# A Mamba block beside an expert layer: expert rows that carry gate and token, expert tiles spread over chunks 1 to 13, low parts on VectorE

## The chip, the cores and the metric

The kernel runs on one core of a Trainium2 chip. The metric is the device time of one execution in microseconds. In what follows VectorE is DVE in the rows, ScalarE is ACT, TensorE is PE (PEld for its weight loads), GpSimd is POOL and SyncE, which issues most DMAs, is SP.

## What is computed

32 sequences of 256 tokens with 128 channels (8192 tokens) are normalized; the result is the input plus the outputs of two branches. All is float32.

```python
xn = layernorm(x)
# branch 1: Mamba, 4 heads of 64 channels, 16 states
x, z  = split(xn @ in_proj_w.T)
x     = silu(causal_conv4(x)); dt_r, B, C = x_proj(x)
delta = softplus(dt_proj(dt_r) + dt_proj_b)
s_t   = s_{t-1} * exp(delta_t * A) + (delta_t * x_t) * B_t
y     = (sum over states of s_t * C_t + x * Dskip) * silu(z)
out1  = y @ out_proj_w.T
# branch 2: 8 experts, each takes at most 1024 tokens (top 1)
gates = softmax(xn @ Wg); e = argmax(gates); slot = place in the expert's queue
hidden = relu(expert_in[e] @ W1[e] + b1[e])
out2[token] = gate * (hidden @ W2[e] + b2[e])[slot]     # 0 when the queue is full
result = x_in + out1 + out2
```

## The kernel before

After a start (normalization, weights, routing) the tokens are worked in 16 chunks of 512 tokens (2 sequences), and a chunk in 32 slots, w = 0 to 31; slots 0 to 15 belong to half 0 of the inner channels, slots 16 to 31 to half 1. Each slot handles 8 channels with 16 states each, on the 128 partitions:

- TensorE spreads delta times x and delta over the states (`spread_du`, L1177, and `spread_delta`, L1184, both float32r) two slots ahead. `spread_delta(w)` goes into one of three banks and waits for scan w-3; `spread_du(w)` goes into one of two and waits for VectorE's product of slot w-2.
- ScalarE makes the decay, exp (L757).
- VectorE makes u = du * B (L897) one slot ahead and the scan of the slot (L967).
- GpSimd multiplies the scan's result by C (L573). In chunk 0 VectorE does three of four of these products (L974), in chunk 15 one of four.
- TensorE sums four slots' products over the states (`sum_quad`, L1199).

Between those stands all other work. Each engine's order is written out: the tables STAGE_A, D_1, OUT_PROJ and FFN give the slot in which TensorE makes each tile, and ScalarE reads it two slots, VectorE one slot, after the last part. All these tiles share two PSUM banks (`misc`) in turn, and `claim` makes TensorE wait until the tile before last was read. STAGE_A is the next chunk's input: x (convolution as four products, L1109), z, bc (B and C), v (L1122) and D (delta, four products, L1130 to L1133), for either half. `outp` is the last chunk's output product (L1142), which VectorE adds to `acc` (`add_out`, L867). The two gate steps of each half (L855, L859) are VectorE's.

Delta goes out as a high and a low part: GpSimd multiplies it by x (`scale_x`, L529) and clears the first step (L533), ScalarE rounds the pair to float32r (`split_high`, L721), and `split_low` takes the difference: on GpSimd in chunks 1 to 8 (L539), on VectorE otherwise (L903). SP then stacks both parts for TensorE (L429).

The experts: in chunk 0 GpSimd scatters the 8192 normalized rows to the experts' queues in HBM with 64 indirect DMAs (L580). Chunks 1 to 8 each work one expert as two halves of 512 rows: transposes `xt` (L1155), four hidden tiles `h` (L1159, ScalarE's relu L732), one output tile `o` in two parts (L1166), which VectorE reads with the bias added (`expert_out`, L875) and SP stores. In chunks 9 to 15 GpSimd gathers the results in token order, 8 indirect DMAs a chunk and 8 more at the end (L549), and VectorE adds each 128-row tile, times its gate, to `acc` (`combine`, L888).

```python
FFN = {"xt0": (18,), "xt1": (19,), "h00": (20,), "h01": (20,), "h02": (21,), "h03": (23,),
       "o0": (24, 24, 25, 25), "h10": (26,), "h11": (26,), "h12": (27,), "h13": (27,),
       "o1": (29, 29, 30, 30)}
SOFTPLUS = {"act": (2, 3, 4, 5), "scale": (9,), "zero": (10,), "low": (13,), "high": (13,)}
```

The numbers of SOFTPLUS are slots after tile v of that half.

Of the kernel before, what the change touches and what calls it, by code (L numbers as in the profile page):

```python
# [1300 lines left out]
```

## Time and profile before

| | us |
|---|---|
| median of 3 runs | 1230.49 (1229.86 to 1234.8) |
| the profiled execution's own time | 1231.65 |
| its span, first to last instruction | 1229.8 |
| VectorE busy | 1065.7 (87%) |
| TensorE busy (weight loads) | 1013.1 (476.6) |
| GpSimd busy | 858.1 (70%) |
| ScalarE busy | 733.5 (60%) |
| mean granted TensorE clock | 0.913 |

The profiled execution is 1.9 us longer than its span; that part lies outside the instructions. A busy TensorE is not one at its peak, since its matmuls are pipelined and their ends are modelled. The 16 chunks begin where the scan of their slot 0 begins: at 93.6, 185.2, 257.6, 325.4, 393.3, 461.1, 529.0, 598.4, 666.3, 734.1, 802.9, 871.3, 939.6, 1007.9, 1076.2 and 1144.4 us.

### The profile page before, as it was taken

To read this page: it belongs to the slowest core of one execution; us is meant where nothing else is said; L and a number is where in the kernel's file an instruction comes from. 1 tells how busy PE (TensorE), PEld (TensorE's weight loads), DVE (VectorE), ACT (ScalarE), POOL (GpSimd) and SP (SyncE) were. 2 spreads that over 40 slices of the span, in tenths; PEclk is the share of its full clock that TensorE was granted. 3 is DMA by queue.
4 is the path that set the end of the run, shared out by engine and by line. 5 is a ranking of instruction groups with operands and counts; after the bars stand their busy time and mean duration, and the time that the engine had idled before them with its cause. 6 is when DMAs were issued, how large, how long until landed. Compare 5 with 4: busy or idle time off the path is not lost.

```text
span 1229.8 us, 12361 instructions
## 1 busy us (share of the span) xinstructions
PE 1013.1 (82%) x3821; PEld 476.6 (39%) x3821; DVE 1065.7 (87%) x1331; ACT 733.5 (60%) x1117; POOL 858.1 (70%) x708
## 2 busy tenths in 40 slices
PE   0755858989999899999899998798888888788775
PEld 0522314444445454444445453243343424243322
DVE  7648968889898979889898989989898989999996
ACT  2563635767585766757685866656664756556421
POOL 2335788767676867677676769687777878787755
PEclk9988878999999999999999998888898979898776
DMA  6542425243533424342534323442434342344311
GB/s 159 160 86 69 98 77 133 58 97 70 120 69 79 103 51 111 78 111 39 117 69 104 85 61 77 86 86 54 87 66 92 80 83 60 80 86 83 75 31 34
DMA packets 81089, 103.36 MB, mean 84 GB/s; under 512 B 13280, under 2 KB 51072, under 8 KB 81024
## 3 DMA queue, kind: packets, MB, share of 16 engines
q1 hardware_dynamic: 76928, 94.18, 35.4%
q0 software_dynamic: 4096, 8.40, 2.3%
q8 instruction: 31, 0.51, 0.2%
q14 instruction: 34, 0.28, 0.1%
HBM read 18.66 MB, written 16.78 MB: 29 GB/s over the span
## 4 chain that ended last, share of the span: by engine, by line
PE 40%; DVE 27%; issue 19%; ACT 6%; POOL 5%; DMA 1%; SPq 1%; POOLq 0%; DVEq 0%; ACTq 0%
DVE u_sb L897 11%; DVE s_sb L967 8%; PE bank L1199 5%; PE bank L1166 5%; PE bank L1184 5%; PE bank L1177 5%; PE bank L1122 3%; PE bank L1109 3%; PE bank L1130 3%; POOL s_sb L573 2%; PE bank L1142 2%; PE bank L1131 2%; PE bank L1132 2%; DVE g_sb L855 2%; DVE g_sb L859 1%
## 5 line engine op out<-in xcount | busy, mean ns | idle before, releaser
L573 POOL TENSOR_TENSOR s_sb<-s_sb,c_of 128x512 f32<-128x512 f32 x480 | 628.1, 1314 | 270.5 <-DVE s_sb L967 266.9
L967 DVE TENSOR_TENSOR_SCAN s_sb<-bank,u_sb 128x512 f32<-128x512 f32 x512 | 619.3, 1210 | 0.0
L757 ACT ACTIVATE bank<-bank,a_neg 128x510 f32<-128x510 f32 x512 | 333.6, 659 | 255.9 <-PE bank L1184 255.0
L897 DVE TENSOR_TENSOR u_sb<-bank,b_of 128x512 f32<-128x512 f32 x512 | 345.2, 674 | 100.8 <-PE bank L1177 100.8
L1177 PE MATMUL bank<-dsp,sel_d 128*128 128x512 f32 x512 | 311.1, 608 | 40.7 <-DVE u_sb L897 21.9
L1184 PE MATMUL bank<-dsp,sel_d 128*128 128x512 f32 x512 | 239.9, 469 | 82.6 <-DVE s_sb L967 77.2
L1177 PEld LDWEIGHTS bank<-dsp,sel_d 128*128 128x128 f32 x512 | 103.1, 201 | 240.4 <-DVE u_sb L897 140.2
L1184 PEld LDWEIGHTS bank<-dsp,sel_d 128*128 128x128 f32 x512 | 104.7, 205 | 196.2 <-DVE s_sb L967 168.9
L1199 PE MATMUL bank<-s_sb,con 128*32 128x512 f32 x1024 | 157.2, 690 | 12.6 <-POOL s_sb L573 8.6
L1109 PE MATMUL bank<-xnT,wx 128*128 128x512 f32 x256 | 129.0, 598 | 0.0
L580 POOL DMA_INDIRECT expert_in<-xn,put_at x64 | 65.4, 1022 | 18.0 <-issue 17.7
L549 POOL DMA_INDIRECT xn<-expert_out,take_now x64 | 65.9, 1030 | 10.6 <-issue 9.1
L721 ACT ACTIVATE hi<-dd 128x1024 fp32r<-128x1024 f32 x32 | 33.9, 1058 | 61.4 <-POOL dd L533 61.4
L1166 PE MATMUL bank<-xn 128*128 128x128 f32 x512 | 63.7, 278 | 7.2 <-ACT xn L732 7.2
L1166 PEld LDWEIGHTS bank<-xn 128*128 128x128 f32 x512 | 60.8, 191 | 18.1 <-ACT xn L732 10.4
L1122 PE MATMUL bank<-xs,bcw 128*64 128x512 f32 x64 | 43.8, 773 | 28.8 <-ACT xs L672 28.8
L529 POOL TENSOR_TENSOR dd<-dd,xs 128x512 f32<-128x512 f32 x32 | 40.8, 1276 | 34.5 <-ACT dd L715 34.5
L1159 PE MATMUL bank<-xn 128*128 128x512 f32 x128 | 64.4, 605 | 0.3
L1109 PEld LDWEIGHTS bank<-xnT,wx 128*128 128x128 f32 x256 | 47.5, 190 | 27.6 <-issue 22.8
L715 ACT ACTIVATE dd<-bank,small 128x512 f32<-128x512 f32 x32 | 22.0, 688 | 57.4 <-PE bank L1133 57.4
L732 ACT ACTIVATE xn<-bank,b_now 128x512 f32<-128x512 f32 x64 | 43.1, 689 | 14.5 <-PE bank L1159 13.9
L1142 PEld LDWEIGHTS bank<-wzo,g_sb 128*128 128x128 f32 x256 | 40.8, 235 | 18.8 <-issue 16.7
(140 smaller groups left out, 1032.1 us busy)
## 6 DMA issues: line engine op xcount, KB each, us to landing
b_of<-bc SPq DMA_DIRECT2D x64, 256.0 KB, 5.5
c_of<-bc SPq DMA_DIRECT2D x64, 256.0 KB, 5.9
dsp<-hi SPq DMA_DIRECT2D x64, 256.0 KB, 4.2
dsp<-dd SPq DMA_DIRECT2D x64, 256.0 KB, 4.7
expert_in<-dd SPq DMA_DIRECT2D x8, 512.0 KB, 6.3
xn<-expert_in SPq DMA_DIRECT2D x8, 512.0 KB, 5.6
xn<-L_ffn_W SPq DMA_DIRECT2D x16, 256.0 KB, 4.8
expert_out<-xn SPq DMA_DIRECT2D x16, 256.0 KB, 2.4
```

What stands on the lines that cost most here:

```text
L549: pool.indirect_dma_start(back[:, n, :], None, eout[:, :], bass.IndirectOffsetOnAxis(ap=take_now[:, n:n + 1], axis=0),).then_inc(S["back_l ...
L573: pool.tensor_tensor(s_now, s_now, c_of[:, hf, hh, :], ALU.mult).then_inc(S["p_ready"], 1)
L580: pool.indirect_dma_start(ein[:, :], bass.IndirectOffsetOnAxis(ap=put_at[:, i:i + 1], axis=0), xn[:, i, :], None).then_inc(S["scattered"], 16)
L757: act.activation(d, d, ACT.Exp, scale=a_neg[:, k:k + 1]).then_inc(S["decay_ready"], 1)
L897: dve.tensor_tensor(u_sb[:, w % U_RING, :], du_ps[w % 2][:, :], b_of[:, hf, head_of(w), :], ALU.mult).then_inc(S["u_ready"], 1)
L967: dve.tensor_tensor_scan(s_sb[:, w % S_RING, :], decay_of(w)[:, :], u_sb[:, w % U_RING, :], 0.0, ALU.mult, ALU.add).then_inc(S["scan_done" ...
L1109: mm = pe.matmul(t[:, :], wx[:, hf, part, :], xnT[:, seqs, part:part + SEQ], start=(part == 0), stop=(part == TAPS - 1))
L1122: pe.matmul(t[0:4 * NS, :] if name[0] == "b" else t[:, :], w[:, hf, :], xs_of(ch, hf), start=True, stop=True).then_inc(S["misc_pe"], 1)
L1166: mm = pe.matmul(t[:, part * P:(part + 1) * P], hT[:, f, part * P:(part + 1) * P], w2_sb[:, f, :], start=(f == 0), stop=(f == FT - 1))
L1177: pe.matmul(du_ps[w % 2][:, :], sel_d[:, group_of(w), :, :].rearrange("k n d -> k (n d)"), dsp[:, hf, head_of(w), 1, :], start=True, stop= ...
L1184: pe.matmul(decay_of(w)[:, :], sel_d[:, group_of(w), :, :].rearrange("k n d -> k (n d)"), dsp[:, w // UNITS, head_of(w), 0, :], start=True ...
L1199: mm = pe.matmul(y_ps[q * 32:(q + 1) * 32, :], con[:, K_SUM + 32 * r:K_SUM + 32 * (r + 1)], s_sb[:, (QUADS * k + q) % S_RING, :], start=(r ...
```

## The change

- **Rows carry their gate and token.** A row of `xn` and of an expert's queue has 130 columns: 128 channels, gate, token number as an integer. Queues are filled first with zero rows whose token number points behind the result (`fill`).
- **Token order by scatter.** ScalarE reads an expert's output tile, now 128 rows wide and one PSUM tile each, and multiplies by the gate (`expert_out`); the bias b2 is added by a product with a row of ones. GpSimd writes each of the 64 tiles to `moe` in token order with an indirect DMA (`put_rows`). SP loads `moe` back in eight pieces after the last expert. GpSimd adds them for chunks 0 to 12 (`add_moe`, one every fourth slot from slot 26 of chunk 13), TensorE for chunks 13 to 15, as four products with the identity inside `out_proj`. The gathers, `combine` and `take_indices` are gone.
- **Tiles in a table of their own.** 144 expert tiles (16 halves of xt, four h, four o) go one by one to the 12 slots of FFN_AT in chunks 1 to 13; two experts' weights and rows are in SBUF at a time. Each tile names its bank, and relu reads its bias without VectorE's copy of it. Stage A and the softplus chain have new slots: D is in two slots, x ends in slot 4.
- **Low parts.** All but the very first are VectorE's, in slot 21 for half 0 and slot 3 of the chunk itself for half 1.

```diff
-LAST_GATHER = 22
+ROWX = DM + 2
...
-STAGE_A = {"z0": (1,), "x0": (2, 4, 5, 7), "bc0": (8,), "v0": (11,), "z1": (12,), "x1": (15, 16, 17, 17),
-           "D0": (18,), "bc1": (25,), "v1": (26,)}
-
-D_1 = (0,)
-OUT_PROJ = (9, 10)
...
+STAGE_A = (
+    ("x0", 1, (0, 1, 3, 4), "act", 6), ("z0", 0, (4,), "act", 5.5), ("bc0", 1, (7,), "bc", 9),
+    ("v0", 1, (9,), "act", 11), ("x1", 1, (11, 12, 13, 14), "act", 16), ("z1", 0, (13,), "act", 15.5),
+    ("D0", 0, (16, 16, 17, 17), "act", 19), ("bc1", 1, (21,), "bc", 23), ("v1", 1, (23,), "act", 25),
+    ("D1", 0, (29, 29, 31, 31), "act", 33))
+FIRST_D1 = (0, (0, 0, 1, 1), "act", 3)
+OUT_PROJ = (1, (18, 19), "dve", 20)
+
+
+FFN_AT = ((2, 0), (7, 0), (9, 0), (11, 0), (19, 0), (21, 0), (23, 0), (25, 0), (26, 1), (27, 0), (28, 1), (30, 1))
+FFN_SKIP = 4
+FFN_LAST_CHUNK = 13
+
+
+SOFTPLUS = ({"act": (11, 12, 13, 14), "scale": (17,), "zero": (18,), "high": (22,), "low": (20,), "low_dve": (21,)},
+            {"act": (25, 26, 27, 28), "scale": (31,), "zero": (32,), "high": (36,), "low": (34,), "low_dve": (35,)})
...
+MOE_ADD_FROM, MOE_ADD_STEP, MOE_ADDS = 13 * 32 + 26, 4, 13
...
-        def low_by_pool(ch):
-
-            return has_ffn(ch)
...
+        def low_by_pool(of):
+
+            return of == 0
...
+            def put_rows(x):
+
+                e, th, q = x.of, x.hf, x.k
+                if x[1:4] == (0, 0, 0):
+                    pool.wait_ge(S["moe_filled"], 16 * EXP)
+                pool.wait_ge(*tile_read(*x[0:4]))
+                pool.indirect_dma_start(moe[:, :],
+                                        bass.IndirectOffsetOnAxis(
+                                            ap=xe[:, e % 2, th * CT + q, DM + 1:ROWX].bitcast(U32), axis=0),
+                                        eo[:, th, q, :], None).then_inc(half_put(e, th)[0], 16)
+
+            def add_moe(k):
+
+                pool.wait_ge(*tile_read("outp", k, 0, 0))
+                pool.wait_ge(S[f"back_loaded{k * CT // GROUP}"], 16)
+                rows = acc[:, k * CT:(k + 1) * CT, :]
+                pool.tensor_tensor(rows, rows, back[:, k * CT:(k + 1) * CT, :], ALU.add).then_inc(S["moe_added"], 1)
...
+            def expert_out(x):
+
+                if x.k == 0 and (x.of, x.hf) != (0, 0):
+                    act.wait_ge(*half_put(x.of - 1 + x.hf, 1 - x.hf))
+                act.wait_ge(S["misc_pe"], tile_made(*x[0:4]))
+                act.activation(eo[:, x.hf, x.k, :], misc[x.bank][:, 0:DM], ACT.Copy,
+                               scale=xe[:, x.of % 2, x.hf * CT + x.k, DM:DM + 1]).then_inc(S["misc_act"], 1)
...
+                    if more:
+                        mm = pe.matmul(t[:, i * P:(i + 1) * P], ident, back[:, ch * CT + i, :],
+                                       start=False, stop=True)
```

How the order moves on TensorE, in chunk 4 from slot 17 on (L1177 and L1184, now L1154 and L1161, are the spreads that open a slot; L1199, now L1176, the sums; L1109 is x, L1155 a transpose of expert rows, L1130 to L1133, now L1089 and L1091, the four products of D, L1103 the output product). Before:

```order
L1177 MATMUL bank<-dsp,sel_d 128x512
L1184 MATMUL bank<-dsp,sel_d 128x512
L1109 MATMUL bank<-xnT,wx 128x512 x2
L1177 MATMUL bank<-dsp,sel_d 128x512
L1184 MATMUL bank<-dsp,sel_d 128x512
L1199 MATMUL bank<-s_sb,con 32x512 x4
L1155 MATMUL bank<-con,xn 128x128 x4
L1130 MATMUL bank<-sp_e,con 128x512
L1131 MATMUL bank<-sp_r,con 128x512
L1132 MATMUL bank<-sp_a,con 128x512
L1133 MATMUL bank<-hi,neg_id 128x512
L1177 MATMUL bank<-dsp,sel_d 128x512
```

And now, from slot 16 on:

```order
L1154 MATMUL bank<-dsp,sel_d 128x512
L1161 MATMUL bank<-dsp,sel_d 128x512
L1089 MATMUL bank<-sp_e,con 128x512
L1089 MATMUL bank<-sp_r,con 128x512
L1154 MATMUL bank<-dsp,sel_d 128x512
L1161 MATMUL bank<-dsp,sel_d 128x512
L1089 MATMUL bank<-sp_a,con 128x512
L1091 MATMUL bank<-hi,neg_id 128x512
L1154 MATMUL bank<-dsp,sel_d 128x512
L1161 MATMUL bank<-dsp,sel_d 128x512
L1176 MATMUL bank<-s_sb,con 32x512 x4
L1103 MATMUL bank<-wzo,g_sb 128x128 x4
```

The sum, the transposes and the whole of D stood in one slot between two pairs of spreads; D now lies in slots 16 and 17, ahead of the sum.

On VectorE, chunk 4, slots 20 to 22 (L897, now L895, is u; L967, now L960, the scan; L855 and L859, now L875 and L879, the gate steps). Before:

```order
L897 TENSOR_TENSOR u_sb<-bank,b_of 128x512
L967 SCALAR_TENSOR_TENSOR s_sb<-bank,u_sb 128x512
L855 SCALAR_TENSOR_TENSOR g_sb<-xs,small,bank 128x512
L897 TENSOR_TENSOR u_sb<-bank,b_of 128x512
L967 SCALAR_TENSOR_TENSOR s_sb<-bank,u_sb 128x512
L859 TENSOR_TENSOR g_sb<-g_sb,zs 128x512
```

And now:

```order
L960 SCALAR_TENSOR_TENSOR s_sb<-bank,u_sb 128x512
L886 TENSOR_TENSOR acc<-bank,acc 128x512
L895 TENSOR_TENSOR u_sb<-bank,b_of 128x512
L960 SCALAR_TENSOR_TENSOR s_sb<-bank,u_sb 128x512
L875 SCALAR_TENSOR_TENSOR g_sb<-xs,small,bank 128x512
L901 TENSOR_TENSOR dd<-dd,hi 128x1024
L895 TENSOR_TENSOR u_sb<-bank,b_of 128x512
```

`add_out` (L886) comes one slot ahead of the first gate step, and the low part (L901) right behind that step.

On GpSimd, from the middle of chunk 3 (L573, now L596, are the products by C; L529, now L542, `scale_x`; L539 the low part; L566 a put). Before:

```order
L573 TENSOR_TENSOR s_sb<-s_sb,c_of 128x512
L533 MEMSET dd 128x2
L573 TENSOR_TENSOR s_sb<-s_sb,c_of 128x512 x3
L539 TENSOR_TENSOR dd<-dd,hi 128x1024
L573 TENSOR_TENSOR s_sb<-s_sb,c_of 128x512 x11
L529 TENSOR_TENSOR dd<-dd,xs 128x512
```

And now:

```order
L596 TENSOR_TENSOR s_sb<-s_sb,c_of 128x512
L546 MEMSET dd 128x2
L596 TENSOR_TENSOR s_sb<-s_sb,c_of 128x512 x2
L566 DMA moe<-xn 8704x128
L596 TENSOR_TENSOR s_sb<-s_sb,c_of 128x512 x2
L566 DMA moe<-xn 8704x128
L596 TENSOR_TENSOR s_sb<-s_sb,c_of 128x512 x2
```

The two low parts of a chunk leave GpSimd, and the puts, each of which waits for ScalarE's copy, stand between its products.

## Rows read from the trace of the kernel before

**Rows 1.** The page: busy time of TensorE to GpSimd; granted clock in 40 slices.

```profile
PE 1013.1 (82%) x3821; PEld 476.6 (39%) x3821; DVE 1065.7 (87%) x1331; ACT 733.5 (60%) x1117; POOL 858.1 (70%) x708
...
PEclk9988878999999999999999998888898979898776
```

**Rows 2.** Stretches: from:to and length, busy (count) by engine, granted clock, DMA share, GB/s.

```profile
93.60:185.20 91.60, 58.09 (x163) 22.98 (x162) 74.95 (x93) 41.38 (x63) 66.92 (x65) 0.80 0.32 79
185.20:257.60 72.40, 66.41 (x277) 33.77 (x276) 60.66 (x73) 47.70 (x74) 54.46 (x44) 0.96 0.39 90
257.60:734.10 476.50, 443.35 (x1919) 227.68 (x1918) 420.35 (x505) 328.52 (x505) 339.49 (x266) 1.00 0.39 86
734.10:1076.20 342.10, 288.55 (x930) 121.97 (x929) 316.18 (x402) 206.29 (x310) 264.43 (x220) 0.87 0.38 78
1076.20:1144.40 68.20, 57.54 (x187) 24.31 (x186) 62.97 (x81) 41.30 (x63) 52.66 (x44) 0.88 0.38 78
1144.40:1213.80 69.40, 50.69 (x147) 19.05 (x145) 67.83 (x86) 21.65 (x33) 47.05 (x39) 0.72 0.23 51
```

**Rows 3.** VectorE's groups, 257.6 to 734.1: busy us, mean ns, idle before, releaser.

```profile
L897 DVE TENSOR_TENSOR u_sb<-bank,b_of 128x512 f32<-128x512 f32 x225 | 151.4, 673 | 46.1 <-PE bank L1177 46.1
...
L875 DVE TENSOR_TENSOR xn<-bank,xn 128x512 f32<-128x512 f32 x14 | 9.5, 676 | 9.5 <-PE bank L1166 9.5
```

**Rows 4.** VectorE's groups, 734.1 to 1076.2.

```profile
L897 DVE TENSOR_TENSOR u_sb<-bank,b_of 128x512 f32<-128x512 f32 x161 | 108.8, 676 | 23.3 <-PE bank L1177 23.3
L888 DVE SCALAR_TENSOR_TENSOR acc<-xn,gate,acc 128x128 f32<-128x128 f32 x40 | 13.0, 326 | 0.0
...
L867 DVE TENSOR_TENSOR acc<-bank,acc 128x512 f32<-128x512 f32 x5 | 3.5, 692 | 2.6 <-PE bank L1142 2.6
```

**Rows 5.** VectorE in order of time, chunk 4: start, us, instruction, idle before.

```profile
393.27 1.21 DVE L967 TENSOR_TENSOR_SCAN s_sb<-bank,u_sb 128x512 f32<-128x512 f32 x1
394.40 0.67 DVE L897 TENSOR_TENSOR u_sb<-bank,b_of 128x512 f32<-128x512 f32 x1
394.99 1.21 DVE L967 TENSOR_TENSOR_SCAN s_sb<-bank,u_sb 128x512 f32<-128x512 f32 x1
...
431.63 0.69 DVE L897 TENSOR_TENSOR u_sb<-bank,b_of 128x512 f32<-128x512 f32 x1 [2.17 <-PE bank L1177]
```

**Rows 6.** TensorE in order of time, chunk 4, slot 18.

```profile
426.90 1.06 PE L1199 MATMUL bank<-s_sb,con 128*32 128x512 f32 x8
...
428.39 1.02 PE L1130 MATMUL bank<-sp_e,con 128*128 128x512 f32 x2
429.26 1.02 PE L1131 MATMUL bank<-sp_r,con 128*128 128x512 f32 x2
...
431.21 0.39 PE L1177 MATMUL bank<-dsp,sel_d 128*128 128x512 f32 x1
```

**Rows 7.** VectorE's low part and GpSimd in order of time, chunk 9.

```profile
748.62 1.27 POOL L573 TENSOR_TENSOR s_sb<-s_sb,c_of 128x512 f32<-128x512 f32 x1
749.39 1.60 DVE L903 TENSOR_TENSOR dd<-dd,hi 128x1024 fp32r<-128x1024 f32 x1
...
750.06 1.79 POOL L549 DMA_INDIRECT xn<-expert_out,take_now  x1 [0.16 <-issue]
```

**Rows 8.** Chunk 0 and the start of chunk 1: VectorE's wait, GpSimd's scatters.

```profile
167.21 1.23 DVE L903 TENSOR_TENSOR dd<-dd,hi 128x1024 fp32r<-128x1024 f32 x1 [9.07 <-ACT hi L721]
...
191.44 0.96 POOL L580 DMA_INDIRECT expert_in<-xn,put_at  x1 [0.30 <-issue]
```

**Rows 9.** The end, in order of time.

```profile
1212.71 2.32 DVE L967 TENSOR_TENSOR_SCAN s_sb<-bank,u_sb 128x512 f32<-128x512 f32 x2
...
1215.61 2.49 POOL L573 TENSOR_TENSOR s_sb<-s_sb,c_of 128x512 f32<-128x512 f32 x2
...
1218.24 1.93 PE L1199 MATMUL bank<-s_sb,con 128*32 128x512 f32 x8 [5.86 <-POOL s_sb L573]
...
1221.85 3.56 PE L1142 MATMUL bank<-wzo,g_sb 128*128 128x128 f32 x16 [1.68 <-DVE g_sb L859]
```

More of the change, by code:

```diff
@@ L53 @@
 GROUP = 8
-FIRST_FFN, FIRST_COMBINE = 1, 9
 EPS = 1e-5
@@ new lines, in expert_tiles, with out_tiles @@
+        def expert_tiles():
+            at = [(c * SLOTS + w, b) for c in range(1, FFN_LAST_CHUNK + 1) for w, b in FFN_AT][FFN_SKIP:]
+            kinds = [("xt", 0)] + [("h", f) for f in range(FT)] + [("o", q) for q in range(CT)]
+            names = [(kind, e, th, k) for e in range(EXP) for th in range(2) for kind, k in kinds]
+            return [Tile(kind, e, th, k, b, (t,), "act", t + 2) for (kind, e, th, k), (t, b) in zip(names, at)]
+        def out_tiles():
+            bank_, slots, by, read = OUT_PROJ
+            tiles = [Tile("outp", c, 0, 0, bank_, tuple((c + 1) * SLOTS + w for w in slots), by,
+                          (c + 1) * SLOTS + read) for c in range(CHUNKS - 1)]
+            end = CHUNKS * SLOTS
+            return tiles + [Tile("outp", CHUNKS - 1, 0, 0, 0, (end, end), by, end)]
@@ new lines, in bass_mamba_moe, with tile_bank @@
+        prior = {}
+        for b in range(2):
+            same = [x for x in plan if x.bank == b]
+            for x, y in zip(same, same[1:]):
+                assert x.slots[-1] <= y.slots[0], (x, y)
+                prior[y[0:4]] = x[0:4]
+        parts_at, reads_at = {}, {}
+        for x in plan:
+            for part, t in enumerate(x.slots):
+                parts_at.setdefault(t, []).append((x, part))
+            reads_at.setdefault(x.read, []).append(x)
+        def tile_bank(*key):
+            return misc[find[key].bank]
@@ new lines, in tile_made, with tile_read @@
+        def tile_made(*key):
+            return made[key]
+        def tile_read(*key):
+            return read[key]
+        def low_by_pool(of):
+            return of == 0
+        events = {}
+        for of in range(CHUNKS):
+            for hf in range(HALVES):
+                slots = {k: tuple((of - 1) * SLOTS + w for w in v) for k, v in SOFTPLUS[hf].items()}
+                if of == 0:
+                    if hf == 0:
+                        continue
+                    slots = {k: (w,) for k, w in FIRST_SOFTPLUS.items()}
+                by_dve_ = of == 0 or not low_by_pool(of)
+                slots.pop("low" if by_dve_ else "low_dve")
+                for what, at in slots.items():
+                    for step, t in enumerate(at):
+                        events.setdefault((what, t), []).append((of, hf, step))
```

742 lines of the change are left out of this document (324 added, 418 removed).

## The prediction

> **What bounds the kernel now.** I read the page's first lines, then stretches by chunk, then VectorE's groups, then single slots. VectorE is the busiest engine [rows 1]; its scans and the making of u cannot be skipped, so the question is what it waits for. One slot without a wait is 394.99 - 393.27 = 1.72 us, and an operation over 512 columns takes 0.59 of that (394.99 - 394.40) [rows 5]. That would be 55.0 us a chunk of 32 slots. The stretches [rows 2] give 476.5 / 7 = 68.1 us for chunks 2 to 8 and 342.1 / 5 = 68.4 us for chunks 9 to 13, almost the same length with different contents. In chunks 2 to 8 VectorE waits for TensorE's next spread and for the expert's output tile: (46.1 + 9.5) / 7 = 7.9 us a chunk [rows 3]. In chunks 9 to 13 it waits (23.3 + 2.6) / 5 = 5.2 us, and spends time on combines [rows 4]. The wait has a place. In slot 18 TensorE goes from the sum at 426.90 through transposes and D to the next spread at 431.21, 4.3 us in one piece [rows 6], and VectorE idles 2.17 us [rows 5]. So a slot may hold 4.3 - 2.2 = 2.1 us of TensorE work beyond its spreads before VectorE feels it, if TensorE came to it on time.
>
> A difference of 0.5% is about what a measurement of this kernel can tell from no change.
>
> **Chunks 2 to 13.** I take VectorE's work without waits from both kinds of chunk, since they must agree.
>
> From chunks 2 to 8: 68.1 - 7.9 = 60.2. Two output tiles leave for ScalarE, 2 x 0.59 = 1.2. Two low parts come from GpSimd, 1.23 each [rows 8], 1.15 in sequence as records overlap by 0.08. That is 60.2 - 1.2 + 2.3 = 61.3.
>
> From chunks 9 to 13: 68.4 - 5.2 = 63.2. Eight combines go, 0.326 each [rows 4], 0.26 in sequence, 2.1 in all; the low parts are VectorE's already. That is 61.1. I use 61.0, since the copies of b1 and of the indices, some tenth each, go too.
>
> Onto this come waits. *TensorE's piles.* One float32 product of 512 columns takes 0.87 (429.26 - 428.39), a sum of four 1.0 [rows 6], a 128-column product at the lower clock 3.56 / 8 = 0.445 [rows 9], so 0.22 at the full one, and an output tile with its bias five of them, 1.1. The 144 expert tiles, 18 a chunk before, are now 11 or 12 a chunk, never two in a slot. The largest run left is slots 14 to 19: x and sum 1.9, none, half of D 1.7, rest of D 1.1, sum and output product 1.9, output product and tile 2.0, with six pairs of spreads near 0.5 in all 11.6 us, where VectorE takes 10.3. It enters with about 1.5 us from slots 11 to 13, so VectorE, which can bear 2.1, waits about 1 us a chunk. Ends: 0, and 5.2 as in chunks 9 to 13; the value is nearer the lower end since the 4.3 us piece is cut in parts under 2.1.
>
> *GpSimd beside VectorE.* At 749.39 a low part began 0.77 us after GpSimd's product and took 1.60 instead of 1.23; GpSimd's next issue took 1.79 [rows 7] where 0.96 is usual [rows 8]. So these two hold each other up when they overlap. In slot 21 the low part now stands behind a gate step of 0.59, by which time the product of the slot is under way: it must wait 0.7 to 0.8. For the other three places (slots 3, 6 and 22) I take 0.5 together, as GpSimd may lag after a put. So 1.3 a chunk; ends 0 and 5.1 (below).
>
> Sum: 61.0 + 1.0 + 1.3 = 63.3, twelve times 759.6 against 476.5 + 342.1 = 818.6: **-59.0 us**.
>
> The Trainium skill says of this in "SBUF — State Buffer", section "SBUF: two separate sides", that VectorE, with two inputs in SBUF, and GpSimd take one port pair exclusively for a whole instruction and that the later one fully blocks. That rule speaks against putting low parts on VectorE; the 1.60 us record agrees with it. Taken at its worst it is the second rival; the sum above holds only the overlap that the order makes certain, and a little more.
>
> **What covers the rest.** GpSimd has 32 products at 1.27 [rows 7], two multiplications of the same size and 64 / 13 = 5 puts at 1.27 (0.96 and a gap of 0.30) [rows 8]: 49.5 of 63.3 us a chunk, since two low parts left it. The puts cost nothing while that slack lasts; if it goes, see the third rival. ScalarE takes 11 or 12 tiles in place of 16 large ones in chunks 2 to 8, and was busy 328.5 / 7 = 46.9 of 68.1 us [rows 2]. SP issues the expert's loads ahead of two stacks; their waits are for puts a chunk old. The eight loads of `moe` run from slot 23 of chunk 13; the first sum on GpSimd, three slots on, may wait a few us once.
>
> **Start, chunk 0 and chunk 1.** Nothing before the first scan at 93.6 moves that I can price over 0.3. In chunk 0 GpSimd issues scatters without pause, and VectorE waits for it, 9.07 us in one place [rows 8]. The low part there is now asked for after slot 19, not 23, but the same 64 scatters stand in GpSimd's queue up to 191.44 + 0.96 = 192.4 [rows 8]. After them now come a multiplication and a product, 2 x 1.27, then ScalarE's rounding and VectorE's low part, 1.2 each (the same 1024 columns). Slot 3 of chunk 1 ends at 197.4 at the earliest. The other 28 slots take 48.2, four gate steps and the sum 3.0, one low part 1.2, small gaps 0.8, waits 2.1: chunk 2 begins at 252.7, not 257.6: **-4.9**. Ends: -9 (no wait behind) and +1.5 (the fills of `moe`, 4 MB more, slow the scatters by a tenth, 64 x 0.1).
>
> **Chunk 14** has no expert tile and the lower clock (0.88) of its kind [rows 2]; waits between 1.0 and 5.2, I take 2.5: 61.0 + 2.5 + 1.3 = 64.8, **-3.4**. **Chunk 15** [rows 2]: 61.0, eight products more (4.7), one low part less (1.2), no scan at the end of the stretch (1.1), waits 1.5: 64.9 for 69.4, **-4.5**. **The end**: the last two products began at 1215.61, behind a gather, though the scans are over by 1215.03 [rows 9]; now the second can end by 1216.6, and the sum begins 1.6 us sooner than at 1218.24. The output product has twelve products for eight, 4 x 0.445 = 1.8 more. **0.**
>
> All in all -4.9 - 59.0 - 3.4 - 4.5 = -71.8 us. The profiled execution took 1231.65, 1.85 of it outside its span; it comes to 1159.9. It stands 1.2 us over the median, so **1159 us**, 5.8% faster.
>
> **Rivals.**
> - *TensorE stays the one waited for.* Banks are now fixed by tile, and a late ScalarE read or a lower clock keeps the waits at the 5.2 us of chunks 9 to 13. Against it: the 4.3 us piece is gone; TensorE, with some 58 of 63 us busy, should keep the clock at 1.00, as it did in chunks 2 to 8 and not in chunks 9 to 13 [rows 2]. 4.2 x 12 = 50 more: 1209 us. Chance 0.10.
> - *Low parts and gate products are blocked in full.* Four VectorE operations a chunk with both inputs in SBUF each wait for a whole product of GpSimd, 4 x 1.27 = 5.1 for 1.3: 3.8 x 13 = 49 more, 1208 us. It needs a GpSimd that is always late. This is the rule of the Trainium skill named above ("SBUF — State Buffer") at its worst. Chance 0.05.
> - *The puts stand on the path (slower).* A put waits on GpSimd for ScalarE's copy, and products queue behind it, which TensorE's sums, and through them everything, wait for. In chunk 0 scatters did this [rows 8]. If each put costs VectorE its whole 1.27, that is 64 x 1.27 = 81 us: 1240 us. It decides from 1.2 us a put on, where the gain is used up. Against it: about five puts a chunk, 6.4 us, against 13.8 us of slack. Chance 0.06.
> - *Nothing is waited for.* The spread-out order takes away all waits: 12 x 2.3 and 7 us elsewhere less, 1124 us. Chance 0.10.
>
> The forecast keeps 0.69; its own range is 1140 to 1180. The range reaches down to most of the last rival and up to part of the first two: 1128 to 1200. Faster by over 0.5%: 0.69 + 0.10 + 0.05 + 0.10 = 0.94. The put rival is split, 0.02 within 0.5%, 0.04 slower.
>
> **What would show it.** Right: chunks 2 to 13 of equal length, 62 to 65 us; VectorE's idle time before u down from 46.1 in seven chunks to under 15; low parts in slot 21 at about 1.9 us, those in slot 3 at 1.23; granted clock 1.00 from chunk 2 to 13; TensorE's sums not waiting for GpSimd. Wrong: idle time before u of 4 us or more a chunk (first rival), every low part near 2.4 (second), GpSimd's products without idle time before them in most slots of chunks 1 to 13 (third), or a chunk under 61.5 us (fourth). Chunk 2 beginning much off 252.7 would show my reading of chunk 0 wrong.

## The result and the profile after

| | before | changed |
|---|---|---|
| median, us | 1230.17 | 1197.48 (1188.55 to 1200.14, 4 runs) |
| ratio to before | | 0.9713, 95% interval 0.9657 to 0.9769 |
| the profiled execution's own time, us | 1231.65 | 1198.12 |
| its span, us | 1229.8 | 1196.3 |
| mean granted clock | 0.913 | 0.920 |

All times are of fast runs; one of the four runs of experiment 12 took 3093.73 us and is left out.

The change makes the kernel 2.9% faster: 33 us, where 71 were forecast. The time lies at the upper end of the range; the direction was right, the size was not.

The page of the changed kernel, busy time and granted clock in 40 slices:

```profile
PE 1016.6 (85%) x3973; PEld 495.0 (41%) x3973; DVE 1077.1 (90%) x1251; ACT 754.5 (63%) x1181; POOL 846.6 (71%) x707
...
PEclk9897858998999998999999899999989999999766
```

It answers to [rows 1]. The stretches of the changed kernel, cut at the same places as [rows 2] (here chunks 2 to 13 are one row):

```profile
95.30:181.90 86.60, 65.37 (x169) 24.89 (x167) 77.39 (x93) 41.77 (x63) 64.05 (x62) 0.74 0.50 130
181.90:257.00 75.10, 63.01 (x230) 29.81 (x228) 61.47 (x72) 45.03 (x71) 55.59 (x47) 0.89 0.40 94
257.00:1055.30 798.30, 735.30 (x3023) 370.04 (x3022) 751.93 (x853) 557.49 (x880) 602.23 (x496) 0.97 0.37 82
1055.30:1118.20 62.90, 54.61 (x198) 23.84 (x196) 61.86 (x72) 41.89 (x63) 53.94 (x45) 0.95 0.45 99
1118.20:1181.70 63.50, 49.89 (x151) 19.27 (x149) 62.53 (x76) 21.56 (x33) 38.75 (x29) 0.68 0.30 71
```

Against the forecast: chunk 2 begins at 257.0 and not 252.7 (+4.3). Chunks 2 to 13 take 798.3 and not 759.6 (+38.7). Chunk 14 takes 62.9 for 64.8, chunk 15 up to the last scan 63.5 for 64.9, and what follows the last scan 14.6 for 16.0 (together -4.7). The sum is 38.3 us, and 1158.05 forecast for the span plus 38.3 is the 1196.3 measured. So the miss is in chunks 2 to 13. VectorE's groups there (busy, mean ns, idle before):

```profile
L960 DVE TENSOR_TENSOR_SCAN s_sb<-bank,u_sb 128x512 f32<-128x512 f32 x384 | 464.3, 1209 | 5.6 <-ACT bank L779 5.6
L895 DVE TENSOR_TENSOR u_sb<-bank,b_of 128x512 f32<-128x512 f32 x385 | 257.8, 670 | 41.4 <-PE bank L1154 40.1
L901 DVE TENSOR_TENSOR dd<-dd,hi 128x1024 fp32r<-128x1024 f32 x24 | 49.4, 2058 | 0.4
```

Waits are (41.4 + 5.6) / 12 = 3.9 us a chunk for a forecast of 1.0. The low parts are (49.4 - 24 x 1.23) / 12 = 1.66 us longer for a forecast of 1.3. With the 61.0 us of work without waits that is 66.6, and 798.3 / 12 is 66.5, so the 61.0 us were right. Waits for TensorE were (46.1 + 9.5) / 7 = 7.9 a chunk before in chunks 2 to 8 [rows 3] and 5.2 in chunks 9 to 13 [rows 4]. They shrank, but did not go. The 5.6 us before scans are waits for ScalarE, 0.47 us in slot 17 of each chunk, behind the loading of a table (chunk 7):

```profile
620.73 1.28 ACT L693 ACT_TABLE_LOAD   x1
622.03 1.81 ACT L779 ACTIVATE bank<-bank,a_neg 128x510 f32<-128x510 f32 x3
...
622.72 1.22 DVE L960 TENSOR_TENSOR_SCAN s_sb<-bank,u_sb 128x512 f32<-128x512 f32 x1 [0.47 <-ACT bank L779]
```

The kernel before had no idle time before its scans. No run tests this wait.

Three readings of the trace say where most of the rest sits. First, slot 3 of chunk 8. In order of time, VectorE and then GpSimd:

```profile
661.98 1.21 DVE L960 TENSOR_TENSOR_SCAN s_sb<-bank,u_sb 128x512 f32<-128x512 f32 x1
663.29 3.65 DVE L901 TENSOR_TENSOR dd<-dd,hi 128x1024 fp32r<-128x1024 f32 x1
666.86 0.68 DVE L895 TENSOR_TENSOR u_sb<-bank,b_of 128x512 f32<-128x512 f32 x1
...
662.12 3.72 POOL L596 TENSOR_TENSOR s_sb<-s_sb,c_of 128x512 f32<-128x512 f32 x3
```

GpSimd, late after a put and a clearing, has three products to catch up. The low part's record begins at 663.29, during the first of them, and ends 1.1 us after the third. The low parts of slot 3 are such in chunks 2, 5, 8 and 11, and 1.50 us in most others; those of slot 21 are 1.9 us throughout. Meanwhile TensorE idles for want of the next u, and its clock falls. Stretches of 6 us around that place (granted clock is the third number from the end):

```profile
658.00:664.00 6.00, 6.00 (x31) 3.31 (x30) 5.89 (x8) 3.82 (x7) 5.44 (x6) 1.00 0.87 164
664.00:670.00 6.00, 4.09 (x10) 1.52 (x9) 6.00 (x5) 4.21 (x6) 4.90 (x4) 0.98 0.43 90
670.00:676.00 6.00, 5.57 (x17) 2.16 (x17) 6.00 (x9) 3.03 (x5) 3.81 (x4) 0.50 0.48 118
```

TensorE was busy 4.09 of 6 us, and then stood at half speed, 1.2 GHz. Second, slot 28 of chunk 7, in order of time:

```profile
645.32 0.65 ACT L723 ACTIVATE sp_e<-sp_e 128x512 f32<-128x512 f32 x1
...
645.84 0.74 ACT L725 ACTIVATE hi<-sp_x,small 128x512 fp32r<-128x512 f32 x1
646.45 0.70 ACT L748 ACTIVATE xn<-bank,b1c 128x512 f32<-128x512 f32 x1
...
647.30 0.46 PE L1126 MATMUL bank<-xn,one_row 1*128 1x128 f32 x2 [2.64 <-ACT xn L748]
...
649.12 0.69 DVE L895 TENSOR_TENSOR u_sb<-bank,b_of 128x512 f32<-128x512 f32 x1 [2.38 <-PE bank L1154]
```

The output tile needs the relu (L748) of the hidden tile one slot ahead of it. ScalarE first does two softplus operations, TensorE stands 2.64 us, and the next spread, behind it in TensorE's order, comes 2.38 us late. Third, the end of every chunk. Chunk 3, TensorE and then VectorE:

```profile
384.49 0.80 PE L1154 MATMUL bank<-dsp,sel_d 128*128 128x512 f32 x1
385.80 0.50 PE L1161 MATMUL bank<-dsp,sel_d 128*128 128x512 f32 x1 [0.51 <-DVE s_sb L960]
386.23 1.07 PE L1176 MATMUL bank<-s_sb,con 128*32 128x512 f32 x8
387.23 1.12 PE L1121 MATMUL bank<-xn 128*128 128x512 f32 x2
387.79 0.79 PE L1154 MATMUL bank<-dsp,sel_d 128*128 128x512 f32 x1
...
388.62 0.69 DVE L895 TENSOR_TENSOR u_sb<-bank,b_of 128x512 f32<-128x512 f32 x1 [1.17 <-PE bank L1154]
```

TensorE waits for the scan that has just ended (three decay banks do not divide 32 slots), then has a sum and a tile before the spread that VectorE needs. This idle time, 1.07 to 1.17 us, stands in slot 31 of eleven of the twelve chunks.

### The profile page after: what moved, and what is told of

Read it like the earlier page. It is cut to its first block, busy times and chain, and to the rows that moved or that the text cites. A ratio compares the mean times of both kernels' runs of the same rounds, so it can differ in the third digit from the quotient of the medians.

```text
span 1196.3 us, 12669 instructions
## 1 busy us (share of the span) xinstructions
PE 1016.6 (85%) x3973; PEld 495.0 (41%) x3973; DVE 1077.1 (90%) x1251; ACT 754.5 (63%) x1181; POOL 846.6 (71%) x707
## 4 chain that ended last, share of the span: by engine, by line
PE 34%; DVE 30%; issue 18%; ACT 9%; POOL 6%; DMA 1%; SPq 1%; POOLq 0%; ACTq 0%; DVEq 0%
DVE u_sb L895 11%; DVE s_sb L960 11%; PE bank L1161 5%; PE bank L1176 4%; PE bank L1129 4%; PE bank L1154 4%; PE bank L1069 4%; POOL expert_in L603 3%; DVE dd L901 3%; PE bank L1080 3%; PE bank L1089 2%; PE bank L1121 2%; ACT bank L779 2%; PE bank L1126 2%; DVE g_sb L875 1%
## 5 line engine op out<-in xcount | busy, mean ns | idle before, releaser
L596 POOL TENSOR_TENSOR s_sb<-s_sb,c_of 128x512 f32<-128x512 f32 x480 | 634.1, 1329 | 221.3 <-DVE s_sb L960 216.8
L960 DVE TENSOR_TENSOR_SCAN s_sb<-bank,u_sb 128x512 f32<-128x512 f32 x512 | 618.7, 1209 | 6.6 <-ACT bank L779 6.6
L895 DVE TENSOR_TENSOR u_sb<-bank,b_of 128x512 f32<-128x512 f32 x512 | 342.8, 669 | 60.5 <-PE bank L1154 59.0
L1154 PE MATMUL bank<-dsp,sel_d 128*128 128x512 f32 x512 | 324.7, 634 | 44.7 <-DVE u_sb L895 31.1
L1161 PE MATMUL bank<-dsp,sel_d 128*128 128x512 f32 x512 | 233.4, 456 | 59.9 <-DVE s_sb L960 57.8
L1154 PEld LDWEIGHTS bank<-dsp,sel_d 128*128 128x128 f32 x512 | 103.0, 201 | 225.5 <-DVE u_sb L895 115.8
L1161 PEld LDWEIGHTS bank<-dsp,sel_d 128*128 128x128 f32 x512 | 103.7, 203 | 175.7 <-DVE s_sb L960 136.6
L1176 PE MATMUL bank<-s_sb,con 128*32 128x512 f32 x1024 | 151.3, 666 | 14.8 <-POOL s_sb L596 11.8
L1069 PE MATMUL bank<-xnT,wx 128*128 128x512 f32 x256 | 132.2, 601 | 0.0
L542 POOL TENSOR_TENSOR dd<-dd,xs 128x512 f32<-128x512 f32 x32 | 40.8, 1275 | 55.6 <-ACT dd L732 55.5
L566 POOL DMA_INDIRECT moe<-xn x64 | 67.9, 1061 | 15.1 <-issue 8.6
L901 DVE TENSOR_TENSOR dd<-dd,hi 128x1024 fp32r<-128x1024 f32 x31 | 60.6, 1956 | 17.5 <-ACT hi L738 17.0
L1129 PE MATMUL bank<-xn 128*128 128x128 f32 x512 | 75.5, 291 | 0.0
L1121 PE MATMUL bank<-xn 128*128 128x512 f32 x128 | 69.5, 626 | 4.3 <-ACT xn L742 4.3
L1129 PEld LDWEIGHTS bank<-xn 128*128 128x128 f32 x512 | 62.9, 194 | 7.8 <-issue 0.2
L748 ACT ACTIVATE xn<-bank,b1c 128x512 f32<-128x512 f32 x64 | 44.4, 694 | 21.0 <-PE bank L1121 20.5
L756 ACT ACTIVATE xn<-bank,xn 128x128 f32<-128x128 f32 x64 | 23.6, 369 | 41.0 <-PE bank L1129 41.0
```

Source lines behind the costliest of these rows:

```text
L596: pool.tensor_tensor(s_now, s_now, c_of[:, hf, hh, :], ALU.mult).then_inc(S["p_ready"], 1)
L895: dve.tensor_tensor(u_sb[:, w % U_RING, :], du_ps[w % 2][:, :], b_of[:, hf, head_of(w), :], ALU.mult).then_inc(S["u_ready"], 1)
L901: dve.tensor_tensor(lo, dd, hi.bitcast(F32), ALU.subtract).then_inc(S["lo_ready"], 1)
L960: dve.tensor_tensor_scan(s_sb[:, w % S_RING, :], decay_of(w)[:, :], u_sb[:, w % U_RING, :], 0.0, ALU.mult, ALU.add).then_inc(S["scan_done" ...
L1069: mm = pe.matmul(t[:, :], wx[:, hf, part, :], xnT[:, seqs, part:part + SEQ], start=(part == 0), stop=(part == TAPS - 1))
L1121: mm = pe.matmul(t[:, :], w1_sb[:, b, x.k * P:(x.k + 1) * P], xeT, start=True, stop=True)
```

## Experiments

Each kernel was timed beside the kernel before on the same chip; that one took 1234.78, 1233.86 and 1232.74 us in the three series (experiments 1 to 4, 5 to 8, 9 to 12). "The changed kernel" is 1197.48, from a series of its own in which the kernel before took 1230.17; it was not timed again. The differences below are of medians. Taken from the ratios instead, experiment 1 gains 8.6 us and not 4.5, experiment 2 24.2 and not 20.9, and the others move by 2.1 us at most.

**1. The decay banks dealt out by the running count.**

```diff
-        def decay_of(w):
-            return decay[w % len(decay)]
+        def decay_of(t):
+            return decay[t % len(decay)]
...
-                last = w - 2 if w >= 3 else (-1, 0, -2)[w]
-                wait(pe, "scan_done", per_chunk(ch, SLOTS, last))
+                t = ch * SLOTS + w
+                wait(pe, "scan_done", t - 2)
```

> The changed kernel with the three decay banks dealt out by the running count of scans, not by the slot in the chunk. Now 32 is no multiple of 3, so the decay spreads issued in slots 30 and 31 wait for the scan that has just begun and not for the one before it. Theory A (fixed places: VectorE's 3.45 us of waits a chunk for TensorE in chunks 2 to 13 sit in a few slots, each with a cause of its own; in slot 31 it is this order): the 1.2 us of idle time before u in slot 31 go in 15 chunks, idle time before u falls from 40.1 to about 26 us in chunks 2 to 13, 1180 us, 1.4% less than the changed kernel. Theory B (TensorE's amount of work is the bound, the place does not matter): the wait turns up in slots 0 to 4, idle time before u stays over 36, 1194 to 1198 us.

Measured: 1193.0 us (1185.7 to 1202.6), ratio 0.9643 (0.9606 to 0.9679). The wait of slot 31 halves, from 1.1 to 0.6 on average, but idle time before u in chunks 2 to 13 is 43.0 us: more stands in slots 27 and 28. By this total and by its time the run is near theory B, though the wait did not turn up in slots 0 to 4. It decides little: its interval and the changed kernel's (0.9657 to 0.9769) overlap, and the profiled execution was the slowest of the four. The clock of the stretch was 0.96, a little under the changed kernel's 0.97 (experiment 9 takes this up).

**2. Both low parts later.**

```diff
-SOFTPLUS = ({"act": (11, 12, 13, 14), "scale": (17,), "zero": (18,), "high": (22,), "low": (20,), "low_dve": (21,)},
-            {"act": (25, 26, 27, 28), "scale": (31,), "zero": (32,), "high": (36,), "low": (34,), "low_dve": (35,)})
+SOFTPLUS = ({"act": (11, 12, 13, 14), "scale": (17,), "zero": (18,), "high": (22,), "low": (20,), "low_dve": (23,)},
+            {"act": (25, 26, 27, 28), "scale": (31,), "zero": (32,), "high": (36,), "low": (34,), "low_dve": (36,)})
```

> The changed kernel with VectorE's low parts asked for in slot 23 instead of 21 and slot 4 instead of 3, where ScalarE's high part has long been ready and no gate step stands between the scan and the low part. Theory A (a low part is long when GpSimd's product is under way as it is asked for): it now starts right behind the scan, level with GpSimd's product; mean of the low parts from 2.06 down to 1.3 to 1.6 us, none at 3.6, 24 x 0.6 = 14 us less in chunks 2 to 13, 1182 us. Rival C (GpSimd gets the port first whenever its product starts together with VectorE's low part): every low part at 1.9 or more, 1190 to 1200 us; the 3.6 us ones (four) go all the same, 4 x 1.7 = 7.

Measured: 1176.58 us (1171.84 to 1177.14), ratio 0.9516 (0.9492 to 0.9541): 20.9 us less than the changed kernel. VectorE's low parts in chunks 2 to 13 of this kernel:

```profile
L901 DVE TENSOR_TENSOR dd<-dd,hi 128x1024 fp32r<-128x1024 f32 x24 | 31.3, 1304 | 0.0
```

That is 49.4 - 31.3 = 18.1 us. Rival C falls: where the low part stands right behind the scan, VectorE gets in ahead of GpSimd's product, in 20 of the 24 places; the other four take 1.8 us. The stretch of chunks 2 to 13 is 16.9 us shorter. Idle time before u stayed (42.6 us for 41.4), so the gain is the low parts' own time. The clock of the stretch rose from 0.97 to 0.98.

**3. Small expert tiles.** For every expert tile TensorE makes only this (its waits stay):

```diff
+                pe.matmul(t[:, 0:32], ident, ident[:, 0:32], start=True, stop=True).then_inc(S["misc_pe"], 1)
```

> The changed kernel with every expert tile on TensorE cut to one product of 32 columns; the tiles' waits, ScalarE's copies and the puts stay. It leaves the experts' arithmetic out. Theory A (fixed places): slot 31 keeps some 1.0 us a chunk for the bank order, the rest of the waits for TensorE falls below 0.5, so 3.45 goes to 1.5, 12 x 2 = 24 us and some 4 in chunk 1 less: 1168 us. Theory B (TensorE's amount of work): waits under 0.5 a chunk, 12 x 3 + 5 = 41 less: 1156 us. If ScalarE's reads alone make the waits: no change, 1190 or more.

Measured: 1166.83 us, ratio 0.9447 (0.9432 to 0.9463). VectorE and the stretch of chunks 2 to 13 in this kernel:

```profile
L895 DVE TENSOR_TENSOR u_sb<-bank,b_of 128x512 f32<-128x512 f32 x385 | 257.7, 669 | 15.6 <-PE bank L1163 14.8
```

```profile
252.90:1025.20 772.30, 683.25 (x2507) 321.43 (x2505) 750.09 (x854) 555.88 (x881) 602.59 (x497) 0.90 0.38 84
```

The time is theory A's, and so is the size of the waits that stay; but they stand in slot 30 (0.6 us a chunk), and slot 31 keeps 0.2 and not 1.0. Idle time before u falls from 41.4 to 15.6 us, but the clock goes down from 0.97 to 0.90: with less to do TensorE gets less often its full clock. So the price of its work is not fixed.

**4. The low parts back on GpSimd.**

```diff
         def low_by_pool(of):
-            return of == 0
+            return True
```

> The changed kernel with all low parts back on GpSimd (slots 20 and 2), one part of the change undone. VectorE loses 2 x 2.06 = 4.1 us a chunk of busy time. Theory A (VectorE's chain with a few fixed waits sets the time): 11 chunks and more at 62.4 to 63.5 instead of 66.5, since GpSimd with 50.2 + 2 x 2.3 = 55 us stays under that: -40 us or so, 1155 us. Theory B (TensorE's amount of work sets it): VectorE only waits more, 1190 us or more. Rival D (GpSimd's low part of over 2 us holds up products, and sums wait for them): 1200 us or more, idle time before TensorE's sums.

Measured: 1193.18 us (1192.91 to 1197.64), ratio 0.9676 (0.9652 to 0.9699): 4 us less than the changed kernel, not 40. Theory B has the time, but no theory had the larger part of the mechanism. VectorE's second gate step in chunks 2 to 13 (658 ns in the changed kernel), and one of them with GpSimd's products, in order of time:

```profile
L879 DVE TENSOR_TENSOR g_sb<-g_sb,zs 128x512 f32<-128x512 f32 x24 | 49.9, 2077 | 0.0
```

```profile
396.67 3.72 POOL L596 TENSOR_TENSOR s_sb<-s_sb,c_of 128x512 f32<-128x512 f32 x3
397.57 3.38 DVE L879 TENSOR_TENSOR g_sb<-g_sb,zs 128x512 f32<-128x512 f32 x1
```

GpSimd's low part (2.37 us) makes it late, and the next VectorE operation with both inputs in SBUF waits until GpSimd has caught up: 49.9 - 15.8 = 34 us take the place of the low parts' 49.4. The waits before u are 55.7 us instead of 41.4. The two together use up what the low parts leave.

**5. The relu of h3 ahead of the softplus step.**

```diff
+                    first = [x for x in reads_at.get(t, []) if x.kind == "h" and x.k == FT - 1]
+                    for x in first:
+                        relu(x)
                     for of, hf_, step in softplus_now(t, "act"):
```

> The changed kernel with one thing moved on ScalarE: where the last hidden tile (h3) of an expert's half and a softplus step fall into one slot, the relu goes first. Theory (pile in slots 25 to 31): in chunks 1, 4, 7 and 10 the output tile of slot 27 follows h3 of slot 26 and TensorE stands up to 2.6 us behind ScalarE's two softplus operations; TensorE's 6.6 us of waits before output tiles go to under 2, VectorE's idle time in slot 28 of those four chunks (2.9, 1.0, 2.4 and 2.4 us) goes to under 0.5 each: 1187 to 1190 us. Rival (TensorE's amount of work; the place only shows it): the time comes back in slots 29 to 31 and 0, no change within 3 us of 1197.

Measured: 1189.06 us (1187.87 to 1193.64), ratio 0.964 (0.962 to 0.966): 8.4 less. Idle time of slot 28 in chunks 1, 4, 7 and 10 is now 1.0, 1.2, 1.2 and 1.1 us instead of 2.9, 1.0, 2.4 and 2.4. Half of it stays, and TensorE still waits 4.4 us for that relu. In this trace something of the rival is seen as well, though not in slots 29 to 31: slot 24 of chunks 5 and 8 now idles 1.7 and 1.4 us, and the total before u is 40.4 for 41.4. The profiled execution was the slowest of the four, at 1193.64 us, so it shows little of the gain; experiment 8 shows it better.

**6. Only the tile of slot 30 small** (the same edit, with the condition `x.slots[0] % SLOTS == 30`).

> The changed kernel with only the expert tile of slot 30 cut to one product of 32 columns (12 or 13 tiles of 144; it leaves their arithmetic out). The banks' order stays. Theory (pile: D in slot 29, sum and tile in slot 30, D in slot 31, 2.6 to 2.8 us of TensorE each with their spreads against 1.72 us of VectorE): the 1.1 us of idle time in slot 31 fall to 0.3 or less, 0.9 x 12 = 11 us less, 1186 us. Rival (the order of the three decay banks alone): slot 31 keeps 0.9 us or more, 1194 to 1198 us.

Measured: 1195.7 us (1189.34 to 1197.96), ratio 0.9692 (0.9651 to 0.9733). Slot 31 falls from 1.1 to 0.4 us, so the tile belongs to that wait. The kernel makes up for little of it: slot 24 of chunks 2, 5 and 11 now idles 1.6 to 1.7 us (0.5 at most in the changed kernel), and the total before u is 35.2 for 41.4. The time is the rival's, the slot the theory's.

**7. Every put twice**, the second time into a tensor that nobody reads (the second issue is shown; the counts of the waits for puts are doubled with it).

```diff
+                pool.indirect_dma_start(moe2[:, :],
+                                        bass.IndirectOffsetOnAxis(
+                                            ap=xe[:, e % 2, th * CT + q, DM + 1:ROWX].bitcast(U32), axis=0),
+                                        eo[:, th, q, :], None).then_inc(half_put(e, th)[0], 16)
```

> The changed kernel with every one of the 64 puts issued a second time, into a second tensor that nobody reads: 64 x 1.06 = 68 us more on GpSimd. If puts stand on the path at their whole price (the slower rival of the prediction): 1255 us or more. If GpSimd's slack covers them: GpSimd has 66.5 - 50.2 = 16.3 us a chunk unused and the second puts take 5 x 1.3 = 6.5, so 1197 to 1203 us, with the low parts of VectorE somewhat longer where GpSimd is later (up to 0.5 x 24 = 12 us, 1209).

Measured: 1213.89 us (1213.56 to 1215.22), ratio 0.9847 (0.9827 to 0.9868): 16.4 us more, 0.26 us a put where the slower rival needed 1.27, and more than the bound of 1209. Chunks 2 to 13 are 17.3 us longer. VectorE now waits up to 2.2 us in slot 3 of eight of these chunks, 14.6 us in all, for the high part, which waits for GpSimd, and its second gate step is longer (21.8 us for 15.8), 2.15 us in slot 6 of four chunks; some low parts are shorter in return:

```profile
L906 DVE TENSOR_TENSOR dd<-dd,hi 128x1024 fp32r<-128x1024 f32 x24 | 45.3, 1889 | 14.6 <-ACT hi L743 14.6
L884 DVE TENSOR_TENSOR g_sb<-g_sb,zs 128x512 f32<-128x512 f32 x24 | 21.8, 910 | 0.0
```

Elsewhere the added work is hidden. From slot 31 to slot 6 of the next chunk GpSimd works half 1's chain of delta beside its products, and there its slack is used up.

**8. Experiments 2 and 5 together.**

> The changed kernel with the later low parts (slots 23 and 4) and the relu of h3 ahead of the softplus step together. If the two gains add: 1176.6 - 9 = 1168 us. If TensorE's amount of work takes over as the bound: 1174 to 1177 us.

Measured: 1166.73 us (1165.72 to 1167.9), ratio 0.9465 (0.9444 to 0.9486). The gains add: 30.8 us for 20.9 + 8.4. Idle time before u in chunks 2 to 13 is 32.9 us, for 42.6 in experiment 2, so the relu brings 9.7 us here. The clock of the stretch is 0.99, and the four runs lie within 2.2 us where those of the changed kernel spread over 11.6.

**9. Experiment 8 with the banks of experiment 1.**

> The kernel with the later low parts and the relu first (1166.7 us) and the decay banks dealt out by the running count of scans as well. Theory (pile: TensorE's work in slots 26 to 31 is 12.1 to 14.5 us against VectorE's 10.3, the bank order only places the wait): slot 31 goes from 1.1 to 0.5 us as it did with the banks alone, up to 0.6 x 13 = 8 us less if TensorE's clock stays: 1159 to 1164 us. Rival (waits only move to slots 27 and 28 of the next chunk, as in the run with the banks alone): 1166 us or more.

Measured: 1156.52 us (1153.36 to 1158.53), ratio 0.9388 (0.936 to 0.9416). The edit whose gain could not be told from the spread of the runs in experiment 1 gives a clear 10.2 us here. VectorE before u and the stretch of chunks 2 to 13:

```profile
L900 DVE TENSOR_TENSOR u_sb<-bank,b_of 128x512 f32<-128x512 f32 x385 | 259.1, 673 | 23.8 <-PE bank L1159 21.9
```

```profile
250.80:1012.90 762.10, 716.64 (x3026) 362.19 (x3025) 733.72 (x854) 559.30 (x881) 605.47 (x494) 1.00 0.38 84
```

The clock is 1.00, and 762.1 / 12 = 63.5 us a chunk. This is the best version, complete, 3.4% under the changed kernel and 6.1% under the kernel before.

**10. D of half 0 in one slot, on top of experiment 8.**

```diff
-    ("D0", 0, (16, 16, 17, 17), "act", 19)
+    ("D0", 0, (17, 17, 17, 17), "act", 19)
```

> The same 1166.7 us kernel with the four products of D of half 0 all in slot 17 instead of two in slot 16 and two in slot 17. This undoes one spreading of the change. By the prediction's reading (a slot may hold 2.1 us beyond its spreads; four products are 3.4) VectorE waits 1.3 us more a chunk, in slots 18 to 20: 15 x 1.3 = 20, 1186 us. If only the sum over the run of slots 14 to 19 counts (unchanged): 1166 to 1169 us.

Measured: 1178.57 us (1177.93 to 1180.19), ratio 0.956 (0.9532 to 0.9587): 11.8 more, 0.8 a chunk. Both readings miss it. Of the 10.6 us in chunks 2 to 13, VectorE idles 0.5 us in slot 19 of every chunk, and 0.5 more in slot 20 of every third. The profiled execution also has 1.7 us in slot 27 of chunks 2 and 11. So the spreading that the change brought is worth 0.6 us a chunk at this place and up to 0.9 with what follows, and the order within the run counts, though less than by the prediction's rule.

**11. Four of the slots 30 left free, on top of experiment 8.**

```diff
+NO_TILE_30 = (1, 2, 4, 5)
...
+                  if not (w == 30 and c in NO_TILE_30)][FFN_SKIP:]
...
-MOE_ADD_FROM, MOE_ADD_STEP, MOE_ADDS = 13 * 32 + 26, 4, 13
+MOE_ADD_FROM, MOE_ADD_STEP, MOE_ADDS = 13 * 32 + 30, 4, 13
```

> The same 1166.7 us kernel, complete, with slot 30 left without a tile in chunks 1, 2, 4 and 5: the expert tiles end four slots of the table later, in chunk 13, and the sums of moe on GpSimd begin four slots later. Theory (pile): the wait of slot 31 (1.1) falls under 0.4 in these four chunks, and no h3 stands one slot ahead of its output tile behind softplus steps in most chunks: 4 x 0.8 + 2 = 5 us less, 1162 us. Rival (less TensorE work lowers its clock, as with the small tiles): 1167 us or more.

Measured: 1177.83 us (1169.27 to 1179.32), ratio 0.9534 (0.9487 to 0.958): 11.1 us more, for the same work in fewer heavy slots. Two chunks make it, 6 and 12, with 71.0 and 69.5 us (63.6 each in experiment 8). Stretches of 6 us in chunk 6:

```profile
552.00:558.00 6.00, 4.14 (x14) 1.80 (x10) 6.00 (x8) 4.36 (x8) 3.96 (x3) 1.00 0.15 31
558.00:564.00 6.00, 6.00 (x22) 3.23 (x23) 5.01 (x6) 4.08 (x7) 4.93 (x5) 0.52 0.61 145
564.00:570.00 6.00, 6.00 (x23) 4.90 (x23) 1.82 (x2) 1.03 (x2) 3.17 (x3) 0.50 0.07 25
570.00:576.00 6.00, 6.00 (x18) 4.04 (x17) 3.65 (x4) 2.06 (x4) 3.39 (x4) 0.56 0.04 18
```

TensorE has little to do behind the low part of slot 23 (4.14 of 6 us). Its clock falls just ahead of slots 25 to 28, which the moved table has filled with the four output tiles of a half, and at half speed it has no idle time left; VectorE was busy 1.82 of 6 us. The rival named the direction. Chunk 9 has the same tiles in the same slots and took 64.9 us. There the clock came back at once:

```profile
758.00:764.00 6.00, 5.73 (x26) 3.07 (x27) 5.36 (x7) 4.53 (x8) 4.67 (x4) 0.72 0.71 164
764.00:770.00 6.00, 6.00 (x37) 4.47 (x36) 4.61 (x6) 3.08 (x6) 5.26 (x6) 1.00 0.06 22
```

So it is the clock at which the pile is met, and not the pile alone, that makes the 6 us.

**12. Only half 1's low part later (slot 4).**

```diff
-            {"act": (25, 26, 27, 28), "scale": (31,), "zero": (32,), "high": (36,), "low": (34,), "low_dve": (35,)})
+            {"act": (25, 26, 27, 28), "scale": (31,), "zero": (32,), "high": (36,), "low": (34,), "low_dve": (36,)})
```

> The changed kernel with only half 1's low part moved, from slot 3 to slot 4; half 0's stays in slot 21. It splits the gain of the run with both (21 us). Theory (a low part that comes while GpSimd has several products to catch up is held 3.64 us, TensorE runs dry meanwhile and its clock falls to half): the four long low parts go, 4 x 2.4, the others of slot 3 give 0.25 x 8, and with them the waits in slots 8 and 24 that follow the low clock, some 2 to 4 us: 13 us less, 1184 us, low parts of slot 21 still 1.9 us. Rival (both places cost alike, 0.65 us each in every chunk): 1187 to 1190 us.

Measured: 1183.68 us (1183.57 to 1185.42, three runs), ratio 0.961 (0.9574 to 0.9646): 13.8 less, near the theory's 13. The low parts of chunks 2 to 13 are 9.7 us shorter; the four long ones now take 1.8 us. The waits of slot 8 went, those of slot 24 did not, and 3.4 us of the gain lie in chunk 1. So slot 3's low parts make some 14 of the 20.9 us of experiment 2, and those of slot 21, all blocked a little, the other 7.

## Why the prediction was off

Its steps one by one.

- **Work without waits, 61.0 us a chunk:** right. 66.5 measured less 3.9 and 1.66 is 60.9; experiment 9 gives 63.5 less (23.8 + 5.6) / 12 of waits and (31.2 - 29.5) / 12 of the low parts, 60.9 again.
- **TensorE's piles, 1.0 us a chunk: this is the step that failed.** All waits together measured 3.9 us. The step took "the largest run left" to be slots 14 to 19 and the bearable pile to be 2.1 us. Slots 14 to 19 cost just its 1.0 us, though only half of it for TensorE: 0.5 before u in slot 15, 0.5 before the scan of slot 17, for ScalarE. The costly run is slots 26 to 31, with 2.0 us a chunk. It holds tiles in 26, 27, 28 and 30, sums in 26 and 30, D in 29 and 31. The text never looked at it. The 2.1 us hold only for a TensorE that comes "on time". At slot 30 it comes with nothing in hand, since the bank order ties it to the scan just ended. Then 0.43 of spread, 1.0 of sum, 0.56 of tile and 0.83 up to u make 2.8 us against VectorE's 1.7, which is the idle time of 1.17 us but for 0.1. The order was in the kernel before too, and in its chunks 9 to 13 VectorE idled 1.8 us in slot 31. And a tile waits on ScalarE's queue, not only on TensorE's work (slot 28).
- **GpSimd beside VectorE, 1.3 us a chunk:** the size was near (1.66), slot 21 right (1.9 forecast and measured), slot 3 wrong: 1.50 in most chunks and 3.6 in four, not 1.23. Behind a long low part TensorE idles and its clock drops: chunks 2 to 13 had 0.97 and not "1.00". What this fall costs by itself is not shown, since in experiment 2 the waits before u stayed as they were.
- **Start and chunk 1, -4.9:** the first scan came 1.7 us later, which I had not priced; its cause stays open. The end of slot 3 of chunk 1 was right, 197.57 for 197.4 at the earliest. The waits behind it were 5.5 us and not 2.1, 2.9 of them the relu's in slot 28.
- **Chunks 14 and 15, the end:** 4.7 us better than forecast; chunk 14 waits 1.0 us and not 2.5.

What the runs put in place of the failed step: the 38.7 us missed in chunks 2 to 13 are 35 us of waits (47.0 for 12) and 4.3 us of low parts, less 0.6. The kernel of experiment 9, with relu and banks mended, has 29.4 us of waits there. So these two faults of order made 17.6 of the 35 us: some 8 to 10 the relu (5, 8), the rest the banks (9). The other 17.4 us stay, spread over slots 12, 15, 17 and 31; of them only the share of TensorE's expert work was tested (experiment 3, which leaves 21.2 us of waits).

The kernel of experiment 9 comes close to the forecast, with 63.5 us a chunk for 63.3 and 1156.5 us in all for 1159. That is luck. It waits 2.45 us a chunk where the sum had 1.0, and its low parts lose 0.14 us where the sum had 1.3; the later low parts took away a cost that the forecast had counted. What mending the same three orders in the kernel before would bring was not tried.

Of the rivals, the first (TensorE stays waited for, 5.2 us a chunk, 1209) describes best what happened: 3.9 us. Its sign, idle time before u of "4 us or more", was missed, at 3.45. Its reasons, banks fixed by tile and a late read by ScalarE, are near what the relu shows, but the bank order that cost was that of the decay banks. The second named the mechanism of the long low parts, but at 1.27 us each and in all four places; the gate products were never blocked in the changed kernel, only in experiments 4 and 7. The trace agrees with the rule of the Trainium skill ("SBUF — State Buffer", section "SBUF: two separate sides") that the pair of ports is held exclusively. It also shows what the rule's words, one whole instruction, do not say: the waiting operation was held for more than one, and at 663.29 and at 397.57 VectorE waited through all products that GpSimd had queued. The third rival is refuted by experiment 7. The fourth had 1124 us; even with three faults mended, waits of 2.5 us a chunk remain.

Of the signs named, idle time before u (41.4 in twelve chunks, 24 in seven, for "under 15") and the clock pointed at the failed step. Equal chunks did too: they run from 64.3 to 68.3 us with a period of three, which is the period of the tile table (nine tiles to an expert's half, 12 slots to a chunk), and that period led to slots 3 and 28.
